# Two transposes of activations and one of gate weights moved from TensorE to VectorE block transposes through DRAM

## What is computed

```
x = x + tanh(g_xattn) * xattn(ctx, layernorm(x))    # keys, values from 77 context tokens
x = x + tanh(g_ffn)   * moe(layernorm(x))

moe(h):                                             # h: (tokens, 128), 16 experts
    logits = normalise(h) @ normalise(sim) - sigmoid(gates)
    mask   = logits > 0, or the two largest where none is
    w      = softmax(relu(logits) where mask)       # (tokens, 16)
    q, k, v = sum_e w[:, e] * (h @ {q,k,v}_proj[e]) # three sums over 16 experts
    o      = softmax(q @ k.T / sqrt(128)) @ v       # within a sequence
    out    = sum_e w[:, e] * (o @ o_proj[e])
```

## Time and profile before

| | |
|---|---|
| three runs | 829.82 to 831.41 us, median 830.87 us |
| the profiled execution | 830.86 us, of it span of the instructions 828.9 us |
| TensorE busy (mean granted clock 0.998) | 793.6 us, 96% |
| VectorE busy | 588.4 us, 71% |
| ScalarE busy | 436.7 us, 53% |
| GpSimd busy | 481.5 us, 58% |
| DMA | 106.40 MB, mean 128 GB/s |
| chain that ended last | TensorE 87%, VectorE 5%, DMA 3%, ScalarE 2% |

### The profile page before, as it was taken

The page is one execution under the profiler, slowest core; times in us unless marked ns, Lnnn a source line. Parts: engine busy times, 40 slices in busy tenths (PEclk is TensorE's granted clock), DMA queues, the critical chain, the costliest instruction groups (busy, mean ns, idle before and its releaser), DMA issues.

```text
span 828.9 us, 13856 instructions
## 1 busy us (share of the span) xinstructions
PE 793.6 (96%) x4111; PEld 432.5 (52%) x4111; DVE 588.4 (71%) x1993; ACT 436.7 (53%) x1134; POOL 481.5 (58%) x702
## 2 busy tenths in 40 slices
PE   5579999999999999999999999999999999999995
PEld 4445555555555555555555555555555555544442
DVE  3777576868588676858768685876868586675647
ACT  4555646456455645645564564556455465544433
POOL 3265656564666656466665646666564665665524
PEclk9999999999999999999999999999999999999999
DMA  7364453544444333444433444543254444334100
GB/s 190 99 227 135 146 197 106 150 149 135 142 141 137 111 103 140 136 142 149 130 115 89 151 132 142 153 135 117 78 160 122 142 153 136 106 94 147 64 7 26
DMA packets 71099, 106.40 MB, mean 128 GB/s; under 512 B 6960, under 2 KB 45552, under 8 KB 71024
## 3 DMA queue, kind: packets, MB, share of 16 engines
q1 hardware_dynamic: 70304, 105.44, 40.5%
q10 hardware_dynamic: 720, 0.08, 0.1%
HBM read 89.51 MB, written 15.99 MB: 127 GB/s over the span
## 4 chain that ended last, share of the span: by engine, by line
PE 87%; DVE 5%; DMA 3%; ACT 2%; POOL 1%; issue 1%; SPq 1%; DVEq 0%; ACTq 0%; POOLq 0%
PE acc_q L1179 19%; PE acc_k L1179 19%; PE acc_v L1179 19%; PE y L1193 9%; PE oT_p L1193 9%; DVE x_all L989 2%; PE m L1307 2%; PE m L1252 2%; PE oT_p L1383 2%; PE m L1293 1%; PE m L1243 1%; PE m L1259 1%; PE m L1300 1%; PE m L1235 1%; PE m L1280 1%
## 5 line engine op out<-in xcount | busy, mean ns | idle before, releaser
L538 POOL TENSOR_TENSOR zq<-zq_full,zq 128x512 f16<-128x512 f32 x256 | 295.4, 1161 | 287.8 <-ACT zq L612 286.0
L612 ACT ACTIVATE zq<-zq_full 128x512 f16<-128x512 f32 x256 | 160.4, 637 | 211.8 <-DVE zq_full L960 209.3
L1179 PE MATMUL acc_q<-zq,w_hi 128*128 128x512 f16 x512 | 194.9, 381 | 2.7 <-POOL zq L538 2.7
L1179 PE MATMUL acc_k<-zq,w_hi 128*128 128x512 f16 x512 | 194.5, 380 | 0.0
L1179 PE MATMUL acc_v<-zq,w_hi 128*128 128x512 f16 x512 | 194.5, 380 | 0.0
L989 DVE SCALAR_TENSOR_TENSOR x_all<-y,w_out,x_all 128x128 f32<-128x128 f32 x356 | 121.8, 342 | 73.8 <-issue 64.9
L960 DVE TENSOR_TENSOR zq_full<-wq_bc,x2T_p 128x512 f32<-128x512 f32 x256 | 167.4, 672 | 3.1 <-DMA wq_bc<-w_rows 2.4
L989 DVE SCALAR_TENSOR_TENSOR x_all<-oT_p,w_out,x_all 128x128 f32<-128x128 f32 x356 | 121.3, 341 | 0.0
L552 POOL TENSOR_TENSOR x_all<-y_sc,x_all 128x128 f32<-128x128 f32 x240 | 100.4, 455 | 19.8 <-DVE x_all L989 13.3
L1179 PE MATMUL acc_q<-zq,w_lo 128*128 128x512 f16 x256 | 97.5, 381 | 0.0
L1179 PE MATMUL acc_v<-zq,w_lo 128*128 128x512 f16 x256 | 97.2, 380 | 0.0
(11 more groups left out here) (191 smaller groups left out, 1113.7 us busy)
## 6 DMA issues: line engine op xcount, KB each, us to landing
wq_bc<-w_rows SPq DMA_DIRECT2D x128, 512.0 KB, 4.4
out_dram<-x_all SPq DMA_DIRECT2D x16, 256.0 KB, 6.7
blk_rows<-v_blk SPq DMA_DIRECT2D x15, 256.0 KB, 4.3
v_mix<-blk_rows SPq DMA_DIRECT2D x60, 64.0 KB, 2.0
blk_rows<-pc_blk SPq DMA_DIRECT2D x15, 256.0 KB, 3.1
pcT<-blk_rows SPq DMA_DIRECT2D x60, 64.0 KB, 2.0
blk_rows<-xn_blk SPq DMA_DIRECT2D x13, 256.0 KB, 2.7
xn_mix<-blk_rows SPq DMA_DIRECT2D x52, 64.0 KB, 3.4
```

Source lines behind the costliest of these rows:

```text
L538: nc.gpsimd.tensor_tensor(zq[:, 1, e % Z_SLOTS, :], zq_full[:, e % F_SLOTS, :], zq[:, 0, e % Z_SLOTS, :], ALU.subtract).then_inc(zq_lo_poo ...
L612: nc.scalar.activation(zq[:, 0, e % Z_SLOTS, :], zq_full[:, e % F_SLOTS, :], ACT.Copy).then_inc(zq_hi_done, 1)
L1179: last = nc.tensor.matmul(acc[m][:], w[:, m, s, :], zq[:, half, s % Z_SLOTS, :], start=(s == 0 and n == 0), stop=(s == E - 1 and n == 2))
```

## The change

- **x2.** For groups from 2 on (`X2_HEAD`), bodies 1 to 14, VectorE transposes `x2` in 32x32 blocks in s2, SyncE writes them to DRAM and reads them back in s3 (one write, four reads), and ScalarE's `x2T_out` copies from `x2_mix` in s5 instead of from PSUM in s2. Group 1 keeps TensorE's transpose, in s4.
- **Gates.** The logit products go from s4 to s6. VectorE's `x2_norm_inverse` goes from s3 to s5, `gate_logits` from s4 to s6, `gate_mask` from s5 to s7, `gate_softmax` from s6 to s8, behind `oT_low`; ScalarE's `gate_exps` from s5 to s7.
- **Weights.** TensorE's `w_transpose` and ScalarE's `wT_out` go. VectorE block-transposes the 64 columns of `w_new` behind softmax, and `weight_rows` is four DMAs (pieces of 128 bytes) for one.
- **px.** For groups from 2 on (`P_HEAD`), bodies 0 to 13, VectorE transposes `px`, padded from 77 to 96 columns, in s11. SyncE writes it and reads it back by three DMAs in s12, behind the store of s11 and the fourth weight transfer, and `pxT_out` copies from `px_mix`.
- **xn.** `xnT_out` for groups from 3 on goes from s5 to s8 on ScalarE, and the four reads of `xn` go behind those of `pcT` on SyncE.
- **Head.** The gate's constants and `first_stats(1)` come before the weights' scales, `second_rstd(1)` and `x2T_move(0)` earlier, the weights' low halves are waited for one projection at a time, and `first_expert` makes the six products with the high half of the input before it waits for the low half.
- **Tail.** In the last group pair 5 is read by VectorE and ScalarE, one bank each, and the pairs' order is changed; the last store is two of half the size.

The core of the diff:

```diff
             def weight_rows(g):
-                wait(sp, wT_sb, g + 1)
-                sp.dma_start(w_rows[bass.ds(g, 1)].rearrange("a r n -> (a r) n"), wT[:]).then_inc(w_rows_in, 16)
-                wait(sp, w_rows_in, 16 * g + 16)
+                wait(sp, w_blk_done, g + 1)
+                for i in range(4):
+                    sp.dma_start(w_rows[g, :, 32 * i:32 * (i + 1)].rearrange("(k c) t -> c k t", k=2),
+                                 w_blk[32 * i:32 * (i + 1)]).then_inc(w_rows_in, 16)
+                wait(sp, w_rows_in, 64 * (g + 1))
...
+                    if s == 3 and X2_HEAD <= g2 < NG:
+                        n = g2 - X2_HEAD
+                        wait(sp, x2_blk_done, n + 1)
+                        wait(sp, x2_mix_in, 64 * n)
+                        blocks_out(3, x2_blk, x2_blk_out)
+                        wait(sp, x2_blk_out, 16 * (n + 1))
+                        wait(sp, x2T_sb, g2)
+                        blocks_in(3, x2_mix, x2_mix_in)
...
+                    if s == 12 and has(g1):
+                        n = g1 - P_HEAD
+                        wait(sp, px_blk_done, n + 1)
+                        wait(sp, px_mix_in, 48 * n)
+                        sp.dma_start(px_rows.rearrange("i t r -> (i t) r"),
+                                     px_blk[:].rearrange("p j b n -> p (j b n)")).then_inc(px_blk_out, 16)
+                        wait(sp, px_blk_out, 16 * (n + 1))
+                        wait(sp, pxT_sb, g1)
+                        for j in range(3):
+                            keys = min(32, S - 32 * j)
+                            sp.dma_start(px_mix[32 * j:32 * j + keys].rearrange("t i b n -> t i (b n)"),
...
             def pxT_out(g):
-                wait(act, pxT_ps, g + 1)
                 wait(act, att_ps, g)
-                nc.scalar.activation(pxT[:], m1[0:S, :], ACT.Copy).then_inc(pxT_sb, 1)
...
+                    wait(act, px_mix_in, 48 * (g - P_HEAD + 1))
...
@@ body on VectorE
+                    if s == 11 and has(g1):
+                        wait(dve, xexp_done, g1 + 1)
+                        wait(dve, px_blk_out, 16 * (g1 - P_HEAD))
+                        blocks_transposed(px_blk, px[:], px_blk_done)
...
-                    if s == 3 and has(g2):
+                    if s == 2 and X2_HEAD <= g2 < NG:
+                        wait(dve, x2_done, g2 + 1)
+                        wait(dve, x2_blk_out, 16 * (g2 - X2_HEAD))
+                        blocks_transposed(x2_blk, x2[:], x2_blk_done)
+                    if s == 5 and has(g2):
                         x2_norm_inverse(g2)
-                    if s == 4 and has(g2):
+                    if s == 6 and has(g2):
                         gate_logits(g2)
-                    if s == 5 and has(g2):
+                    if s == 7 and has(g2):
                         gate_mask(g2)
-                    if s == 6 and has(g2):
-                        gate_softmax(g2)
...
@@ body on TensorE
-                    if s == 2 and has(g2):
+                    if s == 4 and 1 <= g2 < X2_HEAD:
                         x2_transpose(g2)
...
-                    if s == 8 and has(g2):
-                        w_transpose(g2)
...
-                    if s == 12 and has(g1):
-                        px_transpose(g1)
```

More of the change, by code:

```diff
@@ L560, in head @@
                 first_rstd(1)
-                for e in range(LEAD):
+                for e in range(LEAD - 1):
                     zq_low(0, e)
+                second_rstd(1)
+                zq_low(0, LEAD - 1)
                 first_rstd(2)
@@ L567, in body @@
                 for s in range(E):
-                    if s == 0 and has(g2):
+                    if s == 0 and i > 0 and has(g2):
                         second_rstd(g2)
@@ L631, in x2_norm @@
                 wait(act, rstd2_step, 3 * g + 3)
-                wait(act, x2T_ps, g)
+                if g <= X2_HEAD:
+                    wait(act, x2T_ps, g)
+                else:
+                    wait(act, x2_blk_done, g - X2_HEAD)
                 for b in range(G):
@@ L1117, in body @@
                         oT_low(gc)
+                    if s == 8 and has(g2):
+                        gate_softmax(g2)
                     if s == 14 and has(g1):
@@ L1238, in small_product @@
                         last.then_inc(logit_ps, 1)
-                if s == 9 and has(g1):
+                if s == X_SCORES_AT and has(g1):
                     if b == 0:
@@ L1263, in xn_transpose @@
                 wait(pe, xn_done, g + 1)
-                wait(pe, logit_read, cap(g))
+                if g == 2:
+                    wait(pe, x1_done, 2)
                 for b in range(G):
-                    last = nc.tensor.transpose((acc[Q] if g == 1 else m0)[:, tok(b)], xn[:, b, :], ident[:])
+                    last = nc.tensor.transpose((m0, acc[Q], m1)[g][:, tok(b)], xn[:, b, :], ident[:])
                 last.then_inc(xnT_ps, 1)
```

243 lines of the change are left out of this document (145 added, 98 removed).

## The result

The changed kernel takes 859.08 us (median of four runs, 858.63 to 865.27) against 830.86 us: ratio 1.0358, 95% interval 1.031 to 1.0407. The forecast was 849.5 us in a range of 818 to 862. Times here are medians over all executions of a kernel; one of e3's four took 4398.66 us, and the other three have a median of 824.90 us.

A forecast was written before the change was run, and what follows sets the result against it. TensorE's sum of work bounds the middle. Head -3.8, body 0 +0.8, body 1 +4.3, twelve bodies +18.5, body 14 -0.3, tail -0.9 give +18.6 on 830.87: 849.5 us; own range 838 to 862, overall 818 to 862.

The forecast's parts named there:

- The third term, pxT: px's DRAM trip: write lands at 416.0 us behind queued transfers, TensorE's next pair waits, a body grows by 1.54 us.
- 12 x 1.54: Twelve full bodies, 2 to 13, each growing by 1.54 us through the late pxT: 18.5 us.
- Body 0: First body, without output pairs to cover the px trip: +0.8 us, between -0.9 and +3.
- loses 1.7: In body 0, the loss from the uncovered px trip, 1.7 us, set against a win of 0.9.
- Body 1: Body lacking four output pairs, every SyncE step on the path: +4.3 us, between +2.5 and +6.
- The first term, x2T: Before the first logit product in s6: x2's write lands in 2.7 us, TensorE waits 0.25 us.
- The second, the weights: Softmax behind oT's low part: w_blk ready at 403.2 us, weight transfers 2.7 us later, itself hidden.
- the covers: Costs taken as hidden: VectorE's 1.4 us more per body, moved gate steps, SyncE's 11 more issues a body (5 us).
- (1): Rival: transfers keep up, px's write lands before 414, bodies win 0.63 us; 820.5 us, chance 0.22.
- (2): Rival: px lands around 414.5, the wait eats just what TensorE was relieved of; 829.6 us, chance 0.09.
- (3): Rival: x2's write lands in 4.3 us, TensorE stands 1.6 us longer in s6 of 13 bodies; 870 us, 0.07 with (4).
- (4): Rival: moved gate steps meet GpSimd, TensorE waits up to 2 us more in 12 bodies; 873 us, 0.07 with (3).

The follow-up runs named there:

- e3: The changed kernel with px's write and reads on SyncE's queue right behind the first weight transfer, ahead of the other weight transfers and the store; 825.36 us.
- e5: The changed kernel with three weight transfers in front of px's write, and the store and fourth weight transfer behind px's reads; 830.08 us.
- e2: The changed kernel with the x2 transposes back on TensorE in all groups, px still going through DRAM; 872.27 us.
- e10: e3 with x2 and px of group 2 also kept on TensorE, and ScalarE copying oT's high half before rounding that slot's scaled input; 813.86 us.
- e1: The changed kernel with the px transposes back on TensorE in all groups, x2 still going through DRAM; 836.42 us.

## Why the prediction was right, and where its sizes were off

**The third term, pxT, by its steps.** Counted from each body's start, the sum had `px`'s write issued at 35.4 us and landing 6.45 us later; measured 34.85 and 6.5. It had `pxT`'s copy possible at 44.7, and TensorE's pair at 47.5; measured 44.0 and 46.75. So the mechanism, its place and the 6.5 us were right, each step 0.5 to 0.7 us earlier than forecast, and the quiet body grew by 0.83 us where 1.54 was in the sum. e3 and e5 show the queue to be the cause and the landing to decide the sign.

**What made the full bodies grow by 1.87 us in the mean all the same.** The sum knew only one body and one clock. The term that was mis-sized is "12 x 1.54" (18.5 us, measured 22.4): twelve quiet bodies would cost 10.0 us, 8.5 less than the term, and 12.4 us came on top that stood in no term. Of these, 7.5 lie in bodies 6, 10 and 11 (51.4 to 51.6 us each), which have longer waits for `pxT` (1.3 to 1.7 us for 0.35) and then the lower clock; 3.3 lie in bodies 2 to 4, which wait 0.5 to 0.8 us for `x2T` and up to 0.9 for `pxT`; and 1.6 in the other six, with landings of up to 7.3 us. At the rate of e2's two bodies, 1.4 us each, the lower clock alone makes about 4 of the 7.5 us, an estimate. The clock stood in no term, because before the granted clock was 1.00 wherever TensorE worked without a break.

**How the misses add up.** Between the spans the sum was 9.3 us too low (+18.6 for +27.9): head -1.2, body 0 +4.7, body 1 +1.3, the full bodies +3.9, body 14 +1.2, the rest -0.6. That the forecast came out within its own range of 838 to 862 us, by 3 us, owes something to luck: a price for the quiet body that was almost twice too high stood against bodies with a lower clock that the sum did not have.

**Body 0** was put at +0.8, at most +3; it took +5.5. The term that was mis-sized is its "loses 1.7": without output pairs its slots are short, TensorE is at the attention product soon, and nearly the whole landing shows:

```profile
85.81 1.43 PE L1390 MATMUL m<-vx,pxT 77*128 77x128 f32 x5 [4.63 <-ACT pxT L767]
```

4.63 us, and then the lower clock (0.94 in this body). **Body 1** was put at +4.3 and took +5.6. TensorE is idle there for 4.96 of 50.39 us, as the forecast had it ("some 5 us"), before it 1.68. The waits stand before the logits (2.2 us), the attention product and its pair (1.2 and 0.9) and the first output pair (0.7); none is left before `oT_p`, which the forecast named. The other 2.3 us are busy time, at a mean clock of 0.95, which was in no term.

**The first term, x2T.** The write landed in 2.1 us where 2.7 was taken, and the wait was nothing in most bodies where 0.25 was in the sum (its own times, 392.2 and 392.03, give 0.17). That it is 0.5 to 0.8 us in bodies 2 to 4, each with an instruction packet at the reads, was in no rival.

**The second, the weights.** `w_blk` was forecast ready at 29.0 us from the body's start and was written at 28.73; the first weight transfer went out 2.76 us after the first of the four writes, at 31.49 (forecast 32.3). SyncE has 12 more issues a body, not the 11 that the covers name (3 for the weights, 5 for `x2`, 4 for `px`), which changes no term.

**The small terms.** Head -5.0 for -3.8, near its bound of -5.1. Body 14 +0.9 for -0.3: the gates' later steps, counted as covered, delay `oT` there (a wait of 1.6 us for 0.2; e10's edit takes 1.3 us off body 14, and 0.65 in the kernel before). The rest -1.5 for -0.9.

**The rivals.** (1) happened neither here nor by itself, but e3 is its world: quiet bodies of 47.3 us, 0.83 less than before, where it priced 0.63; with body 1 and `x2T` unmended it gave 825, not 820.5. (2) did not happen either; e5 has its time by another way. (3) has its place right and its cause wrong: the write of `x2` lands in 2.1 us, and it is the read behind it that is late, in three full bodies. (4) is there in body 1, not in the full bodies.

## What to carry to other kernels

When work leaves the bounding engine for a trip through DRAM, price the trip with what stands in front of it on the issuing queue: here 6.6, 4.3 or 1.9 us for the same 192 KB write, with 859, 830 or 825 us; then give it a place behind only what is needed sooner, and look at what now waits instead (VectorE, 3.7 us a body in e3, behind four slots of lead). A wait on TensorE costs more than its length if the clock then falls. And an engine that handles two results in program order should not keep the urgent one behind one that has slots to spare (e10).

## What the runs showed of the hardware

- In e1 a 16 KB packet of the instruction queue takes a DMA engine for 0.9 to 1.5 us, and a 64 KB read of `x2` issued within 1 us of it lands 0.7 to 2.7 us later than the others. Its place is tied to the position in TensorE's instruction stream, so that an edit elsewhere in the program moves it onto or off a path: 8.5 us of e1's 836 us went with 40 unused operations in the head.
- In body 6, 2.5 us of idle time in 5.2 went ahead of a mean granted clock of 0.55 in the next 3.8 us; filling the idle time with unused products made e2 9.1 us faster. At like waits body 13 of the changed kernel kept its clock.
- Four writes with pieces of 128 bytes, 8 KB each, cost the queue 1.7 us of issue and landed 1.5 us after issue in the median (the single write of 32 KB before: 0.45 and 1.8 us); the next step was issued 1.0 us after the four issues had ended. The Trainium skill (DMA: Bandwidth & Descriptors, Specifications) wants 512 bytes a descriptor for full rate; no run here shows the rate: at 32 KB in all, what counted was the issue of four writes, the landing was not later.
